# Moving the third output piece of each sequence from the end of the sixth pair to behind the seventh pair's scores

## The reference

```python
x = x + attention(layernorm(x), Wq, Wk, Wv, Wo)     # 16 heads of 64, causal, scores clamped by 50*tanh(s/50)
t = layernorm(x)
shared = gelu(t @ sw1 + sb1) @ sw2 + sb2
probs = softmax(t @ gate_w + gate_b)                # 8 experts, the best 2 of each token are kept
routed = sum over the 2 chosen e of probs[e] * (gelu(t @ w1[e] + b1[e]) @ w2[e] + b2[e])
x = x + routed + shared
```

## Time and profile before

| | |
|---|---|
| median of 3 runs | 1996.77 us (1993.72 to 2000.3) |
| the profiled execution, its own time | 1997.19 us |
| its span in the trace | 1995.5 us |
| PE busy | 1909.4 us, 96% |
| DVE busy | 1536.5 us, 77% |
| ACT busy | 1417.9 us, 71% |
| POOL (GpSimd) busy | 1010.3 us, 51% |
| mean granted PE clock | 0.987 |

### The profile page before, as it was taken

How to read it: one execution, slowest core, us unless ns; L and a number is a source line. 1 busy time by engine, 2 the same in 40 slices (tenths; PEclk the granted TensorE clock), 3 DMA queues, 4 the chain that set the end, 5 groups by cost and what they waited for, 6 DMA issues and landing times.

```text
span 1995.5 us, 40088 instructions
## 1 busy us (share of the span) xinstructions
PE 1909.4 (96%) x14511; PEld 1501.1 (75%) x14511; DVE 1536.5 (77%) x2933; ACT 1417.9 (71%) x2169; POOL 1010.3 (51%) x1195
## 2 busy tenths in 40 slices
PE   6999999999999999999999999999999985998998
PEld 5676777777777777777777777777777764998998
DVE  5678787878778787878788787878787676786776
ACT  6878787878787878777777777777777752454444
POOL 4444555555555555454546463636464542444444
PEclk9999999999999999999999999999999996999999
DMA  3000000000000000010101010101010124765764
GB/s 138 1 21 9 26 23 32 22 33 22 33 22 28 28 20 35 14 42 12 43 12 44 12 43 12 43 12 44 11 44 1 43 75 163 211 208 161 210 196 129
DMA packets 74511, 113.56 MB, mean 57 GB/s; under 512 B 10441, under 2 KB 52942, under 8 KB 74192
## 3 DMA queue, kind: packets, MB, share of 16 engines
q1 hardware_dynamic: 59312, 68.90, 11.6%
q0 software_dynamic: 15008, 42.10, 5.7%
HBM read 64.13 MB, written 48.65 MB: 57 GB/s over the span
## 4 chain that ended last, share of the span: by engine, by line
PE 78%; ACT 15%; DVE 2%; issue 2%; DMA 1%; another core or an unknown queue 1%; SPq 1%; POOL 0%; DVEq 0%; POOLq 0%; ACTq 0%
PE bank_o L1295 12%; PE ring L1199 7%; PE ring L1200 6%; PE ring L1205 6%; PE ring L1272 6%; PE ring L1251 6%; PE ring L1277 5%; ACT prob L607 5%; ACT prob L613 3%; PE ring L1258 3%; PE acc L1319 3%; PE acc L1327 3%; PE acc L1321 3%; PE bank_d L1310 2%; PE acc L1474 1%
## 5 line engine op out<-in xcount | busy, mean ns | idle before, releaser
L523 POOL TENSOR_SCALAR_AFFINE_SELECT prob<-prob 128x256 f32<-128x256 f32 x512 | 223.3, 456 | 646.1 <-ACT prob L613 644.5
L607 ACT ACTIVATE prob<-ring 128x1024 f32<-128x1024 f32 (+1 forms) x384 | 324.7, 875 | 142.7 <-PE ring L1277 136.2
L613 ACT ACTIVATE prob<-prob 128x1024 f32<-128x1024 f32 (+1 forms) x384 | 346.6, 916 | 6.0
L1295 PE MATMUL bank_o<-prob,v 128*32 128x512 f32 (+3 forms) x4096 | 303.4, 436 | 1.2 <-ACT v L603 0.7
L808 DVE TENSOR_TENSOR kT<-ring,kT 64x512 fp32r<-64x512 f32 x256 | 176.3, 689 | 155.4 <-ACT kT L620 152.2
L535 POOL TENSOR_TENSOR key_sum<-prob 128x768 f32<-128x768 f32 x128 | 237.2, 1853 | 74.6 <-PE bank_d L1310 58.1
L1295 PEld LDWEIGHTS bank_o<-prob,v 128*32 128x32 f32 x4096 | 121.8, 110 | 184.9 <-issue 152.1
L1272 PE MATMUL ring<-qT,kT 128*128 128x256 f32 (+3 forms) x1024 | 238.8, 335 | 12.6 <-ACT qT L630 8.8
L822 DVE RECIPROCAL norm<-bank_d 128x512 f32<-128x512 f32 x64 | 214.6, 3353 | 16.8 <-PE bank_d L1310 16.3
L1277 PE MATMUL ring<-q_lo,kT 128*128 128x256 f32 (+3 forms) x1024 | 226.2, 322 | 0.0
L1272 PEld LDWEIGHTS ring<-qT,kT 128*128 128x128 f32 x1024 | 162.8, 189 | 77.4 <-issue 26.5
(11 more groups left out here) (222 smaller groups left out, 4669.1 us busy)
## 6 DMA issues: line engine op xcount, KB each, us to landing
xin<-first SPq DMA_DIRECT2D x71, 257.0 KB
xin<-second SPq DMA_DIRECT2D x71, 129.0 KB
xin<-base SPq DMA_DIRECT2D x71, 128.0 KB
x_next<-in_x SPq DMA_DIRECT2D x16, 512.0 KB, 3.9
x_res<-in_x SPq DMA_DIRECT2D x16, 512.0 KB, 4.0
raw_e<-in_w SPq DMA_DIRECT2D x4, 1024.0 KB, 6.7
first<-pad SPq DMA_DIRECT2D x9, 257.0 KB, 6.7
second<-pad SPq DMA_DIRECT2D x9, 129.0 KB, 6.3
```

What stands on the lines that cost most here:

```text
L523: last = nc.gpsimd.affine_select(out=diag, in_=diag, compare_op=ALU.is_ge, fill=0.0, base=0, pattern=[[0, 2], [1, P]], channel_multiplier=-1)
L607: nc.scalar.activation(probs[p % PROBS][u][:, :, :], slot[:, :, 0:UNIT_COLS[u]], ACT.Tanh, scale=SCALE / SOFTCLAMP).then_inc(act_emptied, 1)
L613: nc.scalar.activation(cols, cols, ACT.Exp, scale=SOFTCLAMP).then_inc(exp_done, 1)
L1295: last = pe.matmul(bank_o[h * QD:(h + 1) * QD, j * P:N], v[:, j, f:f + QD], probs[(2 * quad + h // 2) % PROBS][u][:, h % 2, at:at + N - j ...
```

## The change

`project_out(i, 2)` is taken from the end of the round p = 5, where it stands between `hidden` and `turn_logits`, and put in the round p = 6 behind the three units of scores and ahead of `project_qk(i, 7)`. Nothing else is altered.

```diff
                     for u in UNIT_ORDER:
                         scores(i, p, u)
-                    if p in (5, 7):
+                    if p in (5, 6, 7):
                         project_out(i, p - 4)
...
                     if i >= 1 and p == 5:
                         hidden(i - 1)
-                    if p == 5:
-                        project_out(i, 2)
                     if i >= 1 and p in LATE and (i, p) != COUNT_FIRST:
                         LATE[p](i - 1)
```

## The result

The changed kernel takes 2010.61 us, median of four runs (2007.83 to 2012.99), against 1996.91 us for the kernel before, also of four (1993.72 to 2000.3). The ratio is 1.0059, with a 95% interval from 1.0042 to 1.0076. The profiled execution took 2008.58 us, with a span of 2006.8 us.

What follows compares the result with a forecast made beforehand. PE was taken to bound the first phase, busy 100.11 of 101.25 us per period. 1997.19 + 12.9 - 1.1 = 2009.0 us, with the median 0.4 us lower, gave 2008.6 us; range 2002 to 2014 us.

Steps and rivals of the forecast that it cites:

- The steps of one sequence: From the logits to `turn1` in sequences 1 to 15: 0.86 us more per sequence, 12.9 us in all.
- The hold for the gelu: Ahead of unit 2 of the scores, PE waits 1.19 us for the gelus; some 17 us in the list.
- The wait of the key product: At p = 6 the 0.33 us wait for ACT's clamp goes; L1199's waits fall from 49 to 33.
- The cover: In its old place the 1.46 us output piece hid the gelus and table load, so it cost nothing there.
- Unit 1: Third unit of scores at p = 6: ACT's order keeps its start at 899.93, losing the 0.32 us won earlier.
- the second rival: Unit 1 isn't held by the clamp, so 0.32 us is kept: 7.0 us more, 2003.8 us; chance 0.07.
- the lower bound of its spread: Downstream price if ACT gave up its 0.32 us: -0.32 us per sequence, 15 x 0.32 = 4.8 us down.
- The first sequence: No gelu there, so the scores start 2.2 us earlier; a gain of 1.1 us, once.
- The first (the hold doesn't come): No hold ahead of unit 2, while the key product's wait and restart go: 7.6 us less, 1989 us; chance 0.05.
- The third (the delay is swallowed later): A later wait not hanging on PE takes up the 0.86 us; time stays at 1996 us; chance 0.04.
- The fourth (the clock falls): PE's close stops halve its clock for 6.8 us in each of 15 sequences: 51 us more, 2060 us; chance 0.04.
- The rule weighed: Rotating PSUM banks to overlap evacuation with matmuls; alone it would favour filling the key product's gap, giving 1989 us.

Runs made afterwards that it cites:

- the half: The changed kernel with two of the piece's four token tiles left in the old place, two behind the scores of p = 6; ratio 1.0035.
- the combination: The kernel before with the piece moved in the first sequence alone and unit 0's clamp ahead of unit 2's exponential in p = 3; ratio 0.9987.

## Why the prediction was right

**The forecast** was 2008.6 us, 0.6% slower, and 2010.61 us was measured, inside the range.

**The steps of one sequence** came as worked out. Counted from the gelus' start, unit 2 was to begin after 1.33 us, unit 1 after 3.32, the output piece after 4.51, the key product after 5.97 and `turn1` after 8.78. The trace after has 1.32, 3.32, 4.51, 5.97 and 8.79. The period grew by 0.87 us, against 0.86.

**The hold for the gelu** was to be about 1.2 us, some 17 us in the list; the list has 1.0 and 15.2 us. The end was right, the begin too early: the logits start 0.09 us later against the gelus than I let them, and the list counts from the modelled end of the last matmul.

**The wait of the key product** was to fall to 33 times, and fell to 32. The one too many stands in the first sequence, at 34.98 us of the kernel before (0.22 us). In the changed kernel's trace that product starts at 35.37 us without a wait, behind scores that ran at half the clock, as the last section shows. The run without the table load had the full clock there, and its list has 33. So this one wait is chance, and not the change's.

**The cover** was confirmed from both sides: the piece twice costs nothing more, and the piece anywhere between hidden and the scores costs what it did before.

**Unit 1** starts where ACT's table load lets it, shown by the run without the load. What I gave as the price of this hold, 0.32 us, was too small; the changed kernel pays 0.57 us for it, with the restart. The forecast didn't need that number, since it used unit 1's start directly, but the second rival's time and the lower bound of its spread did: 15 x 0.30 - 1.3 = 3.2 us over the kernel before would have been the rival's true price, not 7.0, and that is some 2000 us, below the range that was to hold it.

**The first sequence** won 1.26 us, against 1.1.

**The rivals.** The first (the hold doesn't come) fell with the wait list. The third (the delay is swallowed later) fell with the period. The fourth (the clock falls) did not occur in the period: the window shows 1.00, and the mean granted clock is 0.987 in both traces. But the row that I held against it does not carry that weight, as the last section shows.

**The rule weighed.** That a group for other PSUM banks should run while a slot is emptied ("Perfetto Trace Analysis" of the Trainium skill, section "Matmuls") fits the traces in both places. It doesn't choose between them; the length of the evacuation does, and here the longer one was left bare. So the 1989 us that I derived from the rule alone is more than the rule says, since it is kept in the old place too.

**What stays open.** The two terms read from the traces give 15 x 0.87 - 1.26 = 11.8 us, and the two profiled executions differ by 2008.58 - 1997.19 = 11.4 us, while the medians differ by 13.7 and 14.6 us. 11.8 us is inside the first interval (8.4 to 15.2 us) and just below the second (12.1 us and up). For the half and the combination, too, the medians lie some 3 us above what the traces give (5.5 against 2.2 us, -1.9 against -4.6 us); for the piece twice they agree (14.1 us both). Behind the last `turn1` the traces vary by more than that where the kernels hardly differ: the stretch up to the experts' first tile takes 171.0 to 174.5 us, and the experts 301.4 to 309.0 us. No run separates these 2 to 3 us.

## What to carry to other kernels

A piece of independent work on the bounding engine is worth what it hides, so before moving it to a wait that the list shows, look up what would be waited for in its old place: that wait isn't in any list, because it is covered. Its length is the distance from the point where the engine would ask to the releaser's end, here 1.1 us against 0.33 us in the new place, and behind the releaser's own work may stand more of it (a table load) that sets the next step. A wait in the list isn't yet a loss: where the engine that is waited for is nearly as late a few steps on, bringing it forward only moves the wait, as at p = 6 here; at p = 3 it won 0.22 us.

## What was not expected of the hardware

The half clock at the start does not follow the same stop each time. Windows of the changed kernel, as in the earlier trace rows:

```profile
21.20:24.60 3.40, 3.40 (x11) 3.01 (x12) 3.37 (x2) 1.72 (x3) 0.70 (x1) 0.50 0.00 0
...
31.50:34.90 3.40, 3.40 (x13) 3.01 (x12) 0.00 (x0) 2.74 (x4) 2.59 (x3) 0.50 0.53 181
```

and the stop ahead of the second, from its timeline of PE:

```profile
31.16 0.51 PE L1272 MATMUL ring<-qT,kT 128*128 128x256 f32 x2 [2.82 <-ACT qT L630]
```

In the kernel before, the same stop (2.63 us) was followed by the full clock, and one stretch of 6.8 us at half came earlier. That earlier stretch stands around the end of a stop of the same length, which my prediction didn't weigh; from the timeline of PE of the kernel before:

```profile
20.77 0.77 PE L1272 MATMUL ring<-qT,kT 128*128 128x256 f32 x2 [2.63 <-DVE q_lo L813]
```

In the changed kernel two stretches of 3.4 us at 1.2 GHz stand there, the second right behind its second stop. The program is the same up to that point in all kernels shown, so their thirteen traces can be put side by side. Around or behind the end of the first stop, of 2.63 us, all thirteen have a stretch at half. Behind the second, nine have another one (stops of 2.69 to 2.84 us) and four have none (2.63 us). So stops of 2.6 to 2.8 us can cost the clock or not, their length alone doesn't tell which, and one row of a stop without a fall was weak evidence. That PE's clock falls back where it idles between bursts is what "TensorE: Matmul & The Clock Gate" of the Trainium skill says in "HAM oscillation — how this bites in real kernels", of waits longer than these. The trace after agrees at 31.5 us, behind a stop of 2.82 us. For the stops of 1.0 us and less in the 15 sequences no fall is seen: the granted clock is 1.00 from 34.9 to 1642.5 us.
